# Attention loops of a two-layer transformer: value products in two halves of the queries in three of four steps, side products cut in halves and put in the middle and at the end of steps

## The chip, the cores and the metric

The kernel runs on one core of one Trainium2 chip. The metric is the time of one execution on the device, in microseconds (us). Lower is better.

## The reference, cut to what matters

The input is 16 sequences of 512 tokens with 256 features. Four layers follow each other, each with a normalisation before it and a residual after it: attention, a feed-forward layer, attention with biases, and a layer of decision trees. The change is in the two attentions:

```
q, k, v = h @ w_q, h @ w_k, h @ w_v         # 16 heads of 16 features
s = (q @ k.T) * scale                       # 512 x 512 for each head
e = exp(s - max(s))                         # layer 0: a maximum for each block of 256 keys
out = (e @ v) / sum(e)                      # then out @ w_o, added to x
```

## The kernel before

Two sequences are worked on as a pair, and there are eight pairs. For each pair the program goes through attention of layer 0 on the first sequence (phase 0), on the second (phase 1), both feed-forward layers (phases 2 and 3), attention of layer 1 on both (phases 4 and 5), and the trees (6 and 7). `attention_even` writes phases 0 and 4, `attention_odd` phases 1 and 5, so each runs 16 times. All five engines have their own written order (one function of the same name for each), and semaphores tie them together.

An attention phase has 16 steps s, one for each head. A step has two **pairs of tiles** (`pair_of_tiles`, L1090), one for each half of the keys. A pair is two times: one product of raw scores for a head that lies seven steps ahead (`maxima`, L1033, matmul L1040), whose row maxima VectorE takes out of PSUM (L753 in layer 0, L756 in layer 1), and one product of this head's scores (`scores`, L1049, matmul L1051), which ScalarE turns into exponentials, 1024 columns at a time (`exps`, L518, activation L524). The raw scores have two banks only, so a tile of them can't be written before VectorE has read the tile before the last. The scores of a half wait for the exponentials of the same half one step back. In `attention_even` the tiles ahead belong to the same phase up to step 8 and to the next phase after that. In `attention_odd` there are none from step 9 on.

Between the first and the second pair of a step stand the **value products** of the group of four heads that is done (`weighted`, L1056, matmul L1065): four matmuls, one for each head of the group, each on 32 columns of the array, over 512 queries. In some steps (`split`) they are done over 256 queries between the pairs and over the other 256 after the second pair. bank 6 collects them; after the fourth step of a group ScalarE reads it (`out_read`, L510), in the middle of that step.

After the second pair stand the **side products** of a step, all into bank 7 or banks that are free:

- `attention_even` makes the queries, keys and values of the next phase: `qk_unit` (matmul L1020, six of 512 columns) and `v_unit` (matmul L1001, twelve of 256 columns). ScalarE reads the queries and keys out twice (`qk_read`, L488, activations L494 and L497), GpSimd makes the low part (`qk_low`, L359), and SyncE stacks both parts with DMAs (`stack_up`, L277, issues L284). In phase 4 VectorE reads the values (L743), in phase 0 ScalarE does (L501).
- `attention_odd` finishes the phase before it: `natural` (transposes L1072, four for each of four token tiles), which VectorE divides (L762 and L764), and `attn_T` (transposes L1077), read by `attn_high` and `attn_low`, then the projection.
- Both transpose the split maxima of four heads into rows (`maxima_rows`, L1043, matmul L1046); ScalarE reads them (`row_read`, L508) and SyncE sends them to the score operands (`rows_up`, L287, issues L290). SyncE does this in a written order: the rows for the first group of the odd phase come after `stack_up` of the fourth query or key unit.

TensorE, VectorE and ScalarE each wait in place: what is queued behind a waiting instruction waits too.

Of the kernel before, what the change touches and what calls it, by code (L numbers as in the profile page):

```python
# [13 lines left out]
T = S // P  # L14
# [4 lines left out]
G = 4  # L19
# [36 lines left out]
def build(nc, t, out):  # L56
    ctx = ExitStack()
    with ctx:
# [413 lines left out]
        def _(act):  # L472
# [54 lines left out]
            def attention_even(b, ph):  # L527
                n, nxt = b * NATT + ATT[ph], ph + 1
                for s in range(H):
                    exps(b, ph, s, 0)  # L530
                    if s % G == 3 and s > 3:
                        out_read(n, ph, s // G - 1)
                    exps(b, ph, s, 1)
                    if s % G == 1:
                        row_read(*((n, (s + 3) // G) if s < 13 else (n + 1, 0)))
                    if s == 0 and nxt == 1:
                        hT_high(b, nxt, 0)
                        hT_high(b, nxt, 1)
                    if s in (2, 3) and nxt == 1:
                        qk_read(n + 1, nxt, s - 2)  # L540
                    if s in (1, 2) and nxt == 5:
                        hT_high(b, nxt, s - 1)
                    if s in (3, 4) and nxt == 5:
                        qk_read(n + 1, nxt, s - 3)
                    if s in (7, 8) and nxt < 4:
                        values(n + 1, nxt, s - 7)
                    if s in (11, 12):
                        qk_read(n + 1, nxt, s - 9)

            def attention_odd(b, ph):  # L550
                n, nxt = b * NATT + ATT[ph], ph + 1
                for s in range(H):
# [3 lines left out]
                    if s % G == 3 and s > 3:  # L556
                        out_read(n, ph, s // G - 1)
                    exps(b, ph, s, 1)
                    if s % G == 1 and s < 13:
                        row_read(n, (s + 3) // G)  # L560
                    if s in (8, 9):
                        attn_high(n - 1, ph - 1, s - 8)
                    if s == 14:
# [400 lines left out]
        def _(pe):  # L964
# [104 lines left out]

            def natural(n, ph, tt):  # L1070
                for g in range(NG):
                    i = nc.tensor.transpose(bank[N_BANK[ph][tt]][:, g * P:(g + 1) * P], oT[:, group_at(ph, g), tt * P:(tt + 1) * P], idf[:])  # L1072
                i.then_inc(nat_ps, 1)

            def attn_T(n, ph, k):
                for tt in range(T):
                    i = nc.tensor.transpose(bank[A_BANK[ph][k]][:, tt * P:(tt + 1) * P], nat_h(ph)[:, tt, k * P:(k + 1) * P], idf[:])  # L1077
                i.then_inc(aT_ps, 1)

# [24 lines left out]
            def attention_even(b, ph):  # L1104
                ai, nxt = ATT[ph], ph + 1
                n = b * NATT + ai
                for s in range(H):
# [4 lines left out]
                    pair_of_tiles(b, ph, n, ahead, s, 0)  # L1112
                    split = s in ((4, 5, 9, 13, 14) if nxt == 1 else (5, 9, 13, 14))
                    if s == G and nxt == 1:
                        pe.wait_ge(qk_sb, (n + 1) * 4 + 1)
                    if s >= G:
                        weighted(n, ai, s // G - 1, s % G, (0,) if split else (0, 1))
                    if s == 0 or (s == 1 and nxt == 5):
                        keep_going(4, bank[6])
# [27 lines left out]
                    if s == 4 and nxt == 5:  # L1147
                        pe.wait_ge(qk_sb, (n + 1) * 4 + 1)
                        qk_unit(n + 1, nxt, 1)
                    if s == 5:  # L1150
                        pe.wait_ge(qk_sb, (n + 1) * 4 + 2)
                        maxima_rows(n, 2)
                    if s == 6:
                        pe.wait_ge(mrow_sb, n * NG + 3)
                        v_unit(n + 1, nxt, 0, 0)
                    if s == 7:
                        v_unit(n + 1, nxt, 0, 1)
                    if s == 8:
                        pe.wait_ge(v_sb, (n + 1) * 2 + 1)
                        v_unit(n + 1, nxt, 1)  # L1160
                    if s == 9:
                        pe.wait_ge(v_sb, (n + 1) * 2 + 2)
                        maxima_rows(n, 3)
                    if s == 10:
                        pe.wait_ge(mrow_sb, n * NG + 4)
                        qk_unit(n + 1, nxt, 2, 0)
                    if s == 11:
                        qk_unit(n + 1, nxt, 2, 1)
                    if s == 12:
                        pe.wait_ge(qk_sb, (n + 1) * 4 + 3)  # L1170
                        qk_unit(n + 1, nxt, 3)
                    if s == 13:
# [3 lines left out]
            def attention_odd(b, ph):  # L1176
                ai, nxt = ATT[ph], ph + 1
                n = b * NATT + ai
                for s in range(H):
# [4 lines left out]
                    pair_of_tiles(b, ph, n, ahead, s, 0)  # L1184
                    split = s in (0, 1, 2, 5)
                    values_of = (n - 1, ai - 1, NG - 1, s) if s < G else (n, ai, s // G - 1, s % G)
                    weighted(*values_of, (0,) if split else (0, 1))
                    pair_of_tiles(b, ph, n, ahead, s, 1)
                    if split:
# [3 lines left out]
                    if s == 3:  # L1193
                        pe.wait_ge(mrow_sb, n * NG + 2)
                        pe.wait_ge(oT_sb, n * NG)
                        natural(n - 1, ph - 1, 0)
                    if s == 4:
                        pe.wait_ge(attn_sb, (n - 1) * T + 1)
                        natural(n - 1, ph - 1, 1)
                    if s == 5:  # L1200
                        pe.wait_ge(attn_sb, (n - 1) * T + 2)
                        maxima_rows(n, 2)
                    if s == 6:
                        pe.wait_ge(mrow_sb, n * NG + 3)
                        natural(n - 1, ph - 1, 2)
                    if s == 7:
                        pe.wait_ge(attn_sb, (n - 1) * T + 3)
                        natural(n - 1, ph - 1, 3)
                    if s == 8:
                        pe.wait_ge(attn_sb, (n - 1) * T + T)  # L1210
                        attn_T(n - 1, ph - 1, 0)
                    if s == 9:
# [318 lines left out]
```

## Time and profile before

| | |
|---|---|
| median of 3 runs | 3346.56 us (3345.4 to 3348.39) |
| profiled execution | 3350.38 us, its span 3348.3 us |
| PE busy | 3053.1 us, 91% of the span |
| DVE busy | 2225.5 us, 66% |
| ACT busy | 1915.2 us, 57% |
| POOL busy | 911.7 us, 27% |
| granted TensorE clock, mean | 0.974 of full speed |

PE is TensorE, DVE VectorE, ACT ScalarE, POOL GpSimd, SPq the DMA issues of SyncE. The table gives shares over all stages. How the engines wait for each other within a step has to be read from the timeline.

### The profile page before, as it was taken

Reading aid. Unit: us, or ns where it says so; the run is one execution under the profiler, and the core shown is the slowest. Engines: PE = TensorE matmul, PEld = TensorE weight load, DVE = VectorE, ACT = ScalarE, POOL = GpSimd, SP = SyncE. Lnnn points to the kernel's source line nnn. Section 1 sums busy time; section 2 is a strip of 40 time slices with the busy share of each in tenths; the row PEclk is TensorE's granted clock in tenths of the full one; section 3 lists DMA queues with packets and bytes.
Section 4 is the critical chain, followed back from the end, with each engine's and each line's share of the span. In section 5 each row is a group of like instructions: output and inputs, shape, how many; then the busy total and the mean of one; then the engine's idle time right before and its main releaser. Section 6 shows DMA issues by size and latency. Waiting matters only on the chain.

```text
span 3348.3 us, 51469 instructions
## 1 busy us (share of the span) xinstructions
PE 3053.1 (91%) x20499; PEld 1392.4 (42%) x20499; DVE 2225.5 (66%) x4099; ACT 1915.2 (57%) x2559; POOL 911.7 (27%) x1206
## 2 busy tenths in 40 slices
PE   0489999999999999999999999999999999999999
PEld 0124355242543436333363434524254343633336
DVE  0785866758566675767667586675856667576764
ACT  0265664747557474565746566474754748456574
POOL 0012323141331414214141232314233141421413
PEclk9689999999999999999999999999999999999999
DMA  3000000000010001000010000100001000100000
GB/s 119 21 22 20 22 27 33 22 20 22 31 38 12 23 19 50 28 2 30 24 39 28 18 24 21 39 22 20 22 29 39 12 22 19 47 28 6 30 18 20
DMA packets 92703, 91.08 MB, mean 27 GB/s; under 512 B 15757, under 2 KB 89877, under 8 KB 92453
## 3 DMA queue, kind: packets, MB, share of 16 engines
q1 hardware_dynamic: 92465, 87.79, 7.7%
q8 instruction: 163, 2.67, 0.3%
q14 instruction: 75, 0.61, 0.1%
HBM read 17.48 MB, written 8.39 MB: 8 GB/s over the span
## 4 chain that ended last, share of the span: by engine, by line
PE 63%; DVE 25%; ACT 5%; SPq 3%; issue 2%; POOL 1%; DMA 1%; DVEq 0%
PE ps L995 13%; PE ps L1040 11%; PE ps L1065 11%; PE ps L1271 8%; DVE nmax L756 8%; DVE nmax L753 8%; PE ps L1001 5%; PE ps L1020 4%; PE ps L1242 3%; PE ps L1051 3%; ACT probs L524 3%; SPq L263 2%; DVE h L734 1%; DVE hT L739 1%; PE ps L1008 1%
## 5 line engine op out<-in xcount | busy, mean ns | idle before, releaser
L524 ACT ACTIVATE probs<-ps 128x1024 f32<-128x1024 f32 x1024 | 1042.8, 1025 | 376.1 <-PE ps L1051 371.9
L1040 PE MATMUL ps<-kst,qst 48*128 48x512 f16 x2048 | 719.1, 394 | 114.0 <-DVE nmax L753 50.5
L753 DVE TENSOR_REDUCE nmax<-ps 128x2 f32<-128x512 f32 x1024 | 651.0, 685 | 196.3 <-PE ps L1040 190.8
L756 DVE TENSOR_REDUCE nmax<-ps 128x1 f32<-128x512 f32 x1024 | 651.2, 685 | 175.7 <-PE ps L1040 172.2
L1051 PE MATMUL ps<-qst,kst 54*128 54x512 f16 x2048 | 697.3, 391 | 5.0 <-ACT probs L524 5.0
L1065 PE MATMUL ps<-probs,vn 128*32 128x512 f32 (+1 forms) x5184 | 577.6, 519 | 6.6 <-ACT oT L512 6.6
L1040 PEld LDWEIGHTS ps<-kst,qst 48*128 48x128 f16 x2048 | 164.4, 93 | 734.1 <-DVE nmax L753 308.0
L420 POOL TENSOR_TENSOR probs<-probs 127x512 f16<-127x512 f32 (+1 forms) x256 | 292.4, 1164 | 519.5 <-ACT probs L655 519.5
L655 ACT ACTIVATE probs<-probs 127x512 f16<-127x512 f32 (+1 forms) x256 | 161.7, 632 | 350.2 <-DVE probs L949 346.8
L1271 PE MATMUL ps<-wout,probs 127*128 127x256 f16 (+1 forms) x3072 | 357.2, 273 | 0.0
L995 PE MATMUL ps<-hT,win 128*127 128x512 f16 (+1 forms) x1536 | 354.3, 380 | 2.7 <-ACT probs L631 2.7
L1271 PEld LDWEIGHTS ps<-wout,probs 127*128 127x128 f16 (+1 forms) x3072 | 297.5, 98 | 55.6 <-issue 10.7
L361 POOL TENSOR_TENSOR parts<-qk,parts 128x512 f16<-128x512 f32 x128 | 149.3, 1168 | 409.8 <-ACT qk L497 408.5
L949 DVE SCALAR_TENSOR_TENSOR probs<-ps,thr,probs 127x512 f32<-127x512 f32 (+1 forms) x256 | 179.8, 744 | 121.5 <-PE ps L1262 121.5
L367 POOL TENSOR_TENSOR npart<-nmax,zero 128x32 f16<-128x32 f32 x128 | 30.7, 239 | 796.3 <-DVE nmax L753 456.5
L995 PEld LDWEIGHTS ps<-hT,win 128*127 128x127 f16 (+1 forms) x1536 | 176.4, 117 | 162.8 <-issue 11.5
L631 ACT ACTIVATE probs<-ps,bin_ 128x512 f32<-128x512 f32 (+1 forms) x256 | 162.4, 682 | 94.8 <-PE ps L995 82.6
L1051 PEld LDWEIGHTS ps<-qst,kst 54*128 54x128 f16 x2048 | 157.7, 93 | 121.9 <-issue 79.2
L571 ACT ACTIVATE probs<-ps 128x512 f32<-128x512 f32 x128 | 76.3, 596 | 218.3 <-PE ps L995 218.1
L382 POOL TENSOR_TENSOR probs<-probs 128x512 f32<-128x512 f32 x128 | 132.9, 1041 | 221.1 <-ACT probs L571 221.1
L1065 PEld LDWEIGHTS ps<-probs,vn 128*32 128x32 f32 x5184 | 103.1, 108 | 211.3 <-issue 152.3
L995 PE MATMUL ps<-hT,wfc 128*128 128x512 f16 x768 | 184.7, 380 | 0.0
(117 smaller groups left out, 3282.0 us busy)
## 6 DMA issues: line engine op xcount, KB each, us to landing
qst<-parts SPq DMA_DIRECT2D x384, 64.0 KB, 2.6
kst<-parts SPq DMA_DIRECT2D x384, 64.0 KB, 2.6
x<-in_x SPq DMA_DIRECT2D x16, 512.0 KB, 3.9
probs<-x SPq DMA_DIRECT2D x16, 512.0 KB, 3.0
out<-probs SPq DMA_DIRECT2D x16, 512.0 KB, 3.0
qst<-nrow SPq DMA_DIRECT2D x256, 12.0 KB
qst<-in_winT SPq DMA_DIRECT2D x1, 2040.0 KB
oT<-in_wfcT SPq DMA_DIRECT2D x1, 1024.0 KB
```

The source lines that it names most:

```text
L420: nc.gpsimd.tensor_tensor(mlo[0:rows, a % 2, leaf, :], masked[0:rows, a % 2, leaf, :], mhi[0:rows, a % 2, leaf, :], ALU.subtract).then_inc ...
L524: nc.scalar.activation(probs[:, g % 2, 2 * hf:2 * hf + 2, s % G, :], ps[:, 2 + 2 * hf:4 + 2 * hf, :], ACT.Exp).then_inc(exp_rd, 1)
L631: nc.scalar.activation(actv[0:rows, a % 2, leaf, :], bank[2 + leaf][0:rows], ACT.Silu, scale=1.0 / WS, bias=bin_[0:rows, a % PAR, leaf:lea ...
L753: nc.vector.tensor_reduce(nmax[:, u, 2 * tt + half, :, slot], bank[tt % 2].rearrange("p (a s) -> p a s", s=BLK), AX.X, ALU.max, negate=Tru ...
L756: nc.vector.tensor_reduce(nmax[:, u, 2 * tt + half, 0, slot:slot + 1], bank[tt % 2], AX.X, ALU.max, negate=True).then_inc(max_rd, 1)
L949: nc.vector.scalar_tensor_tensor(masked[0:rows, a % 2, leaf, :], sel_at(a, leaf)[0:rows], thr[0:rows, leaf:leaf + 1], actv[0:rows, a % 2, ...
L995: ins = mm(out_ps, w[:, a, k, col:col + width], src[:, c, k, :], start=k + i == 0, stop=k == KD - 1 and i == 2)
L1001: ins = mm(out_ps, src[:, c, k, tt * P:(tt + 1) * P], w[:, a, k, :], start=k + i == 0, stop=k == KD - 1 and i == 2)
L1040: mm(bank[tt % 2], qst[lo:hi, ai % 2, e // 2, tt * P:(tt + 1) * P], kst[lo:hi, ai % 2, e // 2, :], start=True, stop=True).then_inc(max_ps, 1)
L1051: i = mm(bank[2 + kt], kst[lo:hi, ai % 2, s // 2, kt * P:(kt + 1) * P], qst[lo:hi, ai % 2, s // 2, :], start=True, stop=True)
L1065: i = mm(bank[6][32 * j:32 * j + 32, lo:hi], vn[:, ai % 2, kt, G * g + j, :], probs[:, g % 2, kt, j, lo:hi], start=kt == 0 and 0 in halves ...
L1271: i = mm(bank[4 + tt // 2][:, tt % 2 * D:(tt % 2 + 1) * D], part[0:rows, a % 2, leaf, tt * P:(tt + 1) * P], wout[0:rows, w, c, leaf, :], s ...
```

## The change

In `attention_even` the value products are cut in halves in the first three of every four steps from step 4 on (before: in steps 5, 9, 13, 14, and 4 in phase 0). The fourth step of a group (7, 11, 15) keeps its 512 queries between the pairs. The side products, which stood at the end of their step, whole or in halves, are now all in halves, one at the end of an even step, the other between the pairs of the odd step after it: value units at 6 and 7, 8 and 9, query and key units 2 and 3 at 10 and 11, 12 and 13, and in phase 4 unit 1 at 4 and 5. Step 7 and step 11 so have 512 queries of values and half a unit between their pairs, and nothing after the second. In `attention_odd` the values are cut in steps 0 to 8 except 3 and 7 (before: 0, 1, 2, 5), and each `natural` and the first `attn_T` is cut in two, the first half at the end of a step and the second between the pairs of the next. ScalarE's reads are moved with the products: for a product that is now complete between the pairs of an odd step, the read stands between the two exponentials of step 9, 13 (and 5 in phase 4), and after both at 7 and 11. GpSimd, VectorE and SyncE keep their order.

```diff
@@ ScalarE, attention_even
+                    if s == 5 and nxt == 5:
+                        qk_read(n + 1, nxt, 1)
+                    if s == 9 and nxt == 1:
+                        values(n + 1, nxt, 1)
+                    if s == 13:
+                        qk_read(n + 1, nxt, 3)
                     exps(b, ph, s, 1)
...
-                    if s in (3, 4) and nxt == 5:
-                        qk_read(n + 1, nxt, s - 3)
-                    if s in (7, 8) and nxt < 4:
-                        values(n + 1, nxt, s - 7)
-                    if s in (11, 12):
-                        qk_read(n + 1, nxt, s - 9)
+                    if s == 3 and nxt == 5:
+                        qk_read(n + 1, nxt, 0)
+                    if s == 7 and nxt == 1:
+                        values(n + 1, nxt, 0)
+                    if s == 11:
+                        qk_read(n + 1, nxt, 2)
@@ ScalarE, attention_odd
+                    if s == 9:
+                        attn_high(n - 1, ph - 1, 0)
                     exps(b, ph, s, 1)
...
-                    if s in (8, 9):
-                        attn_high(n - 1, ph - 1, s - 8)
+                    if s == 9:
+                        attn_high(n - 1, ph - 1, 1)
@@ TensorE
-            def natural(n, ph, tt):
-                for g in range(NG):
+            def natural(n, ph, tt, groups=range(NG)):
+                for g in groups:
...
-            def attn_T(n, ph, k):
-                for tt in range(T):
+            def attn_T(n, ph, k, tts=range(T)):
+                for tt in tts:
@@ TensorE, attention_even
-                    split = s in ((4, 5, 9, 13, 14) if nxt == 1 else (5, 9, 13, 14))
+                    split = G <= s and s % G < G - 1
...
+                    if s == 5 and nxt == 5:
+                        qk_unit(n + 1, nxt, 1, 1)
+                    if s == 7:
+                        v_unit(n + 1, nxt, 0, 1)
+                    if s == 9:
+                        v_unit(n + 1, nxt, 1, 1)
+                    if s == 11:
+                        qk_unit(n + 1, nxt, 2, 1)
+                    if s == 13:
+                        qk_unit(n + 1, nxt, 3, 1)
...
-                        qk_unit(n + 1, nxt, 1)
+                        qk_unit(n + 1, nxt, 1, 0)
...
-                    if s == 7:
-                        v_unit(n + 1, nxt, 0, 1)
                     if s == 8:
                         pe.wait_ge(v_sb, (n + 1) * 2 + 1)
-                        v_unit(n + 1, nxt, 1)
+                        v_unit(n + 1, nxt, 1, 0)
...
-                    if s == 11:
-                        qk_unit(n + 1, nxt, 2, 1)
                     if s == 12:
                         pe.wait_ge(qk_sb, (n + 1) * 4 + 3)
-                        qk_unit(n + 1, nxt, 3)
+                        qk_unit(n + 1, nxt, 3, 0)
@@ TensorE, attention_odd
-                    split = s in (0, 1, 2, 5)
+                    split = s < 9 and s % G < G - 1
...
+                    if s in (4, 5, 7, 8):
+                        natural(n - 1, ph - 1, (s - 4) - (s > 6), (2, 3))
+                    if s == 9:
+                        attn_T(n - 1, ph - 1, 0, (2, 3))
                     pair_of_tiles(b, ph, n, ahead, s, 1)
...
-                        natural(n - 1, ph - 1, 0)
+                        natural(n - 1, ph - 1, 0, (0, 1))
...
-                        attn_T(n - 1, ph - 1, 0)
+                        attn_T(n - 1, ph - 1, 0, (0, 1))
```

## Rows read from the trace of the kernel before

**Rows 1.** The page, costliest groups: busy, mean ns, idle before and its releaser
```profile
L524 ACT ACTIVATE probs<-ps 128x1024 f32<-128x1024 f32 x1024 | 1042.8, 1025 | 376.1 <-PE ps L1051 371.9
L1040 PE MATMUL ps<-kst,qst 48*128 48x512 f16 x2048 | 719.1, 394 | 114.0 <-DVE nmax L753 50.5
```

**Rows 2.** Windows of the third pair: length, busy by engine, granted clock, DMA share
```profile
1000.67:1013.19 12.52, 12.17 (x98) 4.19 (x98) 10.21 (x17) 10.10 (x13) 0.99 (x4) 1.00 0.01 2
1013.19:1028.46 15.27, 13.99 (x110) 3.80 (x111) 12.71 (x21) 13.49 (x18) 3.30 (x6) 1.00 0.16 55
1036.65:1057.92 21.27, 20.00 (x153) 6.60 (x149) 18.16 (x34) 16.58 (x19) 1.98 (x8) 1.00 0.01 3
```

**Rows 3.** Timeline, phase 0, step 7 (start, duration, engine, line, idle before in brackets)
```profile
1000.67 0.39 PE L1040 MATMUL ps<-kst,qst 48*128 48x512 f16 x1
1001.12 0.39 PE L1040 MATMUL ps<-kst,qst 48*128 48x512 f16 x1
1001.44 1.06 PE L1065 MATMUL ps<-probs,vn 128*32 128x512 f32 x8
1002.44 0.39 PE L1040 MATMUL ps<-kst,qst 48*128 48x512 f16 x1
1002.66 0.38 PE L1040 MATMUL ps<-kst,qst 48*128 48x512 f16 x1
...
1002.86 2.59 DVE L753 TENSOR_REDUCE nmax<-ps 128x2 f32<-128x512 f32 x4 [0.48 <-PE ps L1040]
1002.97 0.83 PE L1001 MATMUL ps<-wv,hT 128*128 128x256 f16 x6
...
1003.74 0.39 PE L1040 MATMUL ps<-kst,qst 48*128 48x512 f16 x1
```

**Rows 4.** Timeline, phase 0, steps 13 to 15: values over 256 queries, and a row transposition
```profile
1022.08 0.64 PE L1065 MATMUL ps<-probs,vn 128*32 128x256 f32 x8
...
1022.54 0.39 PE L1046 MATMUL ps<-idb,npart 128*24 128x128 f16 x4
...
1022.86 0.39 PE L1040 MATMUL ps<-kst,qst 48*128 48x512 f16 x1
...
1024.94 0.64 PE L1065 MATMUL ps<-probs,vn 128*32 128x256 f32 x8
...
1025.52 0.39 PE L1040 MATMUL ps<-kst,qst 48*128 48x512 f16 x1
```

**Rows 5.** Timeline, phase 0, step 3: a pair of tiles with nothing before it
```profile
989.22 1.89 DVE L753 TENSOR_REDUCE nmax<-ps 128x2 f32<-128x512 f32 x3 [2.33 <-PE ps L1040]
...
989.97 0.39 PE L1040 MATMUL ps<-kst,qst 48*128 48x512 f16 x1 [0.35 <-DVE nmax L753]
...
990.57 0.39 PE L1040 MATMUL ps<-kst,qst 48*128 48x512 f16 x1 [0.21 <-DVE nmax L753]
```

**Rows 6.** Timeline, feed-forward stage: values over 512 queries, then full-array matmuls
```profile
1081.87 1.06 PE L1065 MATMUL ps<-probs,vn 128*32 128x512 f32 x8
...
1082.87 1.05 PE L1242 MATMUL ps<-wpt,probs 128*128 128x256 f16 x8
```

**Rows 7.** Timeline, ScalarE, SyncE and TensorE from the fourth unit to phase 1
```profile
1020.10 0.60 ACT L494 ACTIVATE parts<-ps 128x512 f16<-128x512 f32 x1 [0.35 <-PE ps L1020]
...
1021.74 3.78 SPq L284 DMA_DIRECT2D kst<-parts  x6
1025.57 34.54 SPq L290 DMA_DIRECT2D qst<-nrow  x8
...
1028.46 0.39 PE L1040 MATMUL ps<-kst,qst 48*128 48x512 f16 x1 [0.71 <-DMA qst<-nrow]
```

**Rows 8.** Timeline, phase 1, step 4: VectorE's division and TensorE's transposes; eight transposes
```profile
1041.34 0.25 DVE L762 RECIPROCAL rden<-ps 128x16 f32<-128x16 f32 x1
...
1042.10 0.66 PE L1072 MATMUL ps<-idf,oT 128*128 128x128 f32 x4
...
1042.70 0.39 PE L1040 MATMUL ps<-kst,qst 48*128 48x512 f16 x1
...
1071.11 1.09 PE L1008 MATMUL ps<-idf,h 128*128 128x128 f32 x8
```

More of the change, by code:

```diff
@@ L1068, in weighted @@
                     i.then_inc(pv_step, 1)
-            def natural(n, ph, tt):
-                for g in range(NG):
+            def natural(n, ph, tt, groups=range(NG)):
+                for g in groups:
                     i = nc.tensor.transpose(bank[N_BANK[ph][tt]][:, g * P:(g + 1) * P], oT[:, group_at(ph, g), tt * P:(tt + 1) * P], idf[:])
-                i.then_inc(nat_ps, 1)
-            def attn_T(n, ph, k):
-                for tt in range(T):
+                if g == NG - 1:
+                    i.then_inc(nat_ps, 1)
+            def attn_T(n, ph, k, tts=range(T)):
+                for tt in tts:
                     i = nc.tensor.transpose(bank[A_BANK[ph][k]][:, tt * P:(tt + 1) * P], nat_h(ph)[:, tt, k * P:(k + 1) * P], idf[:])
-                i.then_inc(aT_ps, 1)
+                if tt == T - 1:
+                    i.then_inc(aT_ps, 1)
             def projected(n, ph, half):
@@ L1195, in attention_odd @@
                         pe.wait_ge(oT_sb, n * NG)
-                        natural(n - 1, ph - 1, 0)
+                        natural(n - 1, ph - 1, 0, (0, 1))
                     if s == 4:
                         pe.wait_ge(attn_sb, (n - 1) * T + 1)
-                        natural(n - 1, ph - 1, 1)
+                        natural(n - 1, ph - 1, 1, (0, 1))
                     if s == 5:
@@ L1204, in attention_odd @@
                         pe.wait_ge(mrow_sb, n * NG + 3)
-                        natural(n - 1, ph - 1, 2)
+                        natural(n - 1, ph - 1, 2, (0, 1))
                     if s == 7:
                         pe.wait_ge(attn_sb, (n - 1) * T + 3)
-                        natural(n - 1, ph - 1, 3)
+                        natural(n - 1, ph - 1, 3, (0, 1))
                     if s == 8:
                         pe.wait_ge(attn_sb, (n - 1) * T + T)
-                        attn_T(n - 1, ph - 1, 0)
+                        attn_T(n - 1, ph - 1, 0, (0, 1))
                     if s == 9:
```

## The prediction

> **What bounds the kernel now.** I first read the costliest groups of the page. ScalarE's exponentials idle 376 us, nearly all of it waiting for TensorE's scores; TensorE idles 114 us before the raw score tiles, the largest part released by VectorE's maxima [rows 1]. So TensorE sets the pace of the attention phases, and VectorE can hold it. The windows give the length of the stretches that the change touches, all at the full clock: 12.52 us for steps 7 to 10 of phase 0, 15.27 from step 11 to the start of phase 1, 21.27 for steps 3 to 9 of phase 1 [rows 2]. Last I read single steps in the timeline, for the distances between starts. I count from the first tile of a pair:
>
> - pair: second tile 0.22 later, and the next block 0.32 after the second tile [rows 3].
> - values over 512 queries: 1.00 until the next pair [rows 3]; over 256: 0.58, taken as 0.57 [rows 4].
> - half a side product (six matmuls of 256 columns; three of 512 are the same work): 0.77 until the next pair [rows 3]. Row transposition: 0.32 [rows 4].
> - VectorE starts 0.42 after the pair's first tile when idle [rows 3]. After a read starts, TensorE may write the next tile 0.75 later, and the second tile 1.35 later [rows 5]; I use 0.73 and then steps of 0.62 (2.59 for four tiles, less their tail).
>
> Applied to steps 7 to 10 before, these distances give 3.07 (the start of step 7 to that of step 8 [rows 3]), then a step with a whole unit, a split one with row transposition, and a full one; they sum to the 12.5 of the window [rows 2]. In the old step 7 both halves are full: 0.45 + 0.32 + 1.00 = 1.77 and 0.22 + 0.31 + 0.77 = 1.30. VectorE needs 1.24 for two tiles, is idle 0.48 of each step, and holds TensorE 0.22 once [rows 3].
>
> **The change part by part.** Nothing is taken away: the matmul columns are the same, only four more matmul instructions stand where values are cut, whose cost is in the distances below. What changes is distribution.
>
> (a) Price of a cut. Two halves of values take 2 × 0.57 = 1.14 against 1.00 where each is followed by another kind of matmul. No row shows a half followed by a full-array product. It is followed by a row transposition after 0.46 [rows 4]; 512 queries are followed by a full-array product after 1.00 [rows 6], the same as by a pair [rows 3]. So I take 0.57, and keep 0.46 as the lower bound. The Trainium skill (TensorEngine Tiling (Array Packing), Key Properties) says that changing the tiling mode drains TensorE. By that rule the half pays its drain before a side product too, and the sum would be the higher one below; without it, the lower one.
>
> (b) Steps 6 and 10 of the even phases (cut values, half a unit at the end). Pair at 0, values 0.54; the next pair could come at 1.11, but VectorE began at 0.42 and frees the banks at 1.16 and 1.78. So values at 2.10, side half at 2.67, end at 3.44. Before: 0.54 + 1.00 + 0.55 + 0.77 = 2.86. Costs 0.58 in step 6, where TensorE's waits are back between the pairs and VectorE then idles at the end.
>
> (c) Steps 7 and 11 (512 queries and half a unit in the middle, nothing at the end). Values 0.55, side half 1.55, second pair 2.32, its second tile 2.55. VectorE, idle meanwhile, begins at 2.74, so the next step's pair has its tiles at 3.47 and 4.09, as a pair after a pair in rows 5. Values of step 8 then start at 4.41, where TensorE's work alone would allow 3.4. Step 7 takes 3.47 instead of 3.07.
>
> (d) Steps 8 and 9. From there: second pair 4.98 and 5.33, values 5.65, side half 6.22, step 9 at 6.99; values 7.54, side half 8.11, pair 8.88, values 9.43, rows 9.89, step 10 at 10.20. Here is the gain: the whole unit and the waiting of the old split step 9 are spread. But (c) eats it. Step 10 by (b), with its pair delayed to 10.65: step 11 at 13.63, against 12.52 [rows 2]. +1.1.
>
> (e) Steps 11 to the odd phase. The same up to step 14 (unit 3 ends in the middle of step 13). Its second half starts at 8.11 and ScalarE reads from 8.98, with 0.60 and 0.49 for the two reads; the row transposition behind waits for them until 10.1 and step 14 starts at 10.4. For the DMAs: in the old phase the read of unit 3 starts at 1020.10, the six issues at 1021.74, since SyncE is still busy with unit 2; the rows go out at 1025.57 and TensorE starts phase 1 at 1028.46, released by that DMA [rows 7]. Now: high part ready 9.58, six issues of together 3.8, rows out at 13.4, TensorE 2.9 later at 16.3, against 15.27 [rows 2]. TensorE and VectorE alone would be there at 15.9. +1.0. Queued behind the waiting tile is all of step 0.
>
> Even phase of layer 0: steps 4 and 5 as before, 0.58 + 1.1 + 1.0 = 2.7. Phase 4 has the same and unit 1 in halves at steps 4 and 5: one more cut (0.3), and the row transposition of step 5 now waits for two reads of ScalarE that begin only after the middle product (0.4): 3.4. VectorE's reads of the values there sit in stretches in which it idled; I price them at nothing, 0.2 if that cover fails.
>
> (f) Odd phases, steps 3 to 9. Four transposes take 0.60 until the pair [rows 8]; from eight (1.09) against four (0.66) a half is about 0.45 [rows 8]. Four products are cut in two (+0.3 each, five with attn_T), and values cut in steps 4, 6, 8 (+0.14 each). What VectorE had hidden: in step 4 nothing is lost to the values, but the second pair slips behind the half transposition, VectorE divides (from 1041.34 [rows 8]; about 0.62 until its next tile) and the tiles behind it come later. Worked through from step 3: steps 4 to 10 start at 2.95, 6.30, 9.39, 12.59, 15.90, 19.43 and, since the row transposition of step 9 now waits for ScalarE's and VectorE's reads of the first attn_T (made in the middle of the step), 23.1, against 21.27 [rows 2]. +1.8; with 0.46 and a half transposition at 0.33, +0.8. From step 10 on the work is the same and TensorE-bound; nothing is given back.
>
> **Sum.** 2.7 + 3.4 + 2 × 1.8 = 9.7 us for a pair of sequences, × 8 = 78 us. On the profiled execution's 3350.4: 3428. The median of the runs lies 3.8 below it, so 3424. Bounds: with the low prices 1.9 + 2.3 + 2 × 0.8 = 5.8, × 8 = 46, 3393; with a SyncE chain of 4.5 instead of 3.8 and 2.2 in an odd phase 3.4 + 3.7 + 4.4 = 11.5, × 8 = 92, 3439.
>
> **Rivals.**
>
> (A) Faster. The single waits of TensorE for a bank, 0.2 to 0.4 us in steps 7, 8, 9, 11, 12 and 13 of an even phase (1.6 together; the 0.22 of step 7 is in rows 3), vanish because cut values keep VectorE supplied earlier, while the six cuts cost 0.14 each: -0.8 for a phase, × 32 phases = -26 us, 3321. It decides for this if a bank is free when TensorE comes back, thus if VectorE lags less than 1.1 behind a pair. For: VectorE idles 0.48 in a step [rows 3], scores come sooner, and ScalarE waits for them [rows 1]. Against: rows 5 show 1.35 until the second tile.
>
> (B) No change. What TensorE loses in (b) and (c) it regains in (d), since VectorE's and TensorE's totals are the same and the cuts hide in waits: 3346. For: steps 8 and 9, taken alone, are as long as before. Against: (c) leaves a pair against a pair, a wait that no other work covers, and the odd phases have no such pair to regain from.
>
> (C) Slower through the clock. TensorE is now about 85% busy in steps where it was 93%. If the granted clock falls to 1.2 GHz in steps 7 and 11, the matmuls after it double for a while: a lost 1.1 us for each six matmuls, twice in each of 32 phases, +70 on top: 3490. Against: the clock is 1.00 in all three windows, split steps with waits among them [rows 2].
>
> **How the numbers follow.** Forecast 0.80 (slower by 46 to 92), C 0.06, A 0.08, B 0.06. Slower by over 0.2% (6.7 us, about what a measurement of this kernel can tell from no change): 0.86; within 0.2%: 0.06; faster: 0.08. The range runs from 3375, below the low prices, since one of the waits may be covered, to 3450.
>
> **What would show it.** In the changed profile, step 7 of phase 0: after the second pair VectorE starts 0.42 later, and the next pair's tiles follow 1.15 and 1.77 after the pair, released by VectorE; steps 7 to 10 last 13.6. TensorE's idle before L1040 grows from 114 us to some 170. Phase 1 starts 16.3 after step 11, released by the DMA of the rows. Half values to half a unit: 0.57 (right) or 0.46. Steps 3 to 9 of the odd phase: 23 instead of 21.3. I am wrong if step 7 is 3.1 or less, or if the banks are free when TensorE comes back from half the values.

## The result, and the profile after

The changed kernel takes 3427.8 us (median of 4, 3424.0 to 3434.6) against 3347.5 us: slower by a factor of 1.0231 (95% interval 1.0214 to 1.0247), 80 us. The forecast was 3424, of a range of 3375 to 3450. The profiled execution of the changed kernel took 3431.0 us, its span is 3428.9 us.

The page of the changed kernel, busiest engines and the groups that answer to those of [rows 1] (busy, mean ns, idle before and its releaser):

```profile
PE 3098.3 (90%) x21459; PEld 1403.2 (41%) x21459; DVE 2231.0 (65%) x4099; ACT 1923.1 (56%) x2559; POOL 911.8 (27%) x1206
...
L524 ACT ACTIVATE probs<-ps 128x1024 f32<-128x1024 f32 x1024 | 1042.3, 1026 | 436.2 <-PE ps L1059 432.8
L1048 PE MATMUL ps<-kst,qst 48*128 48x512 f16 x2048 | 718.7, 397 | 137.3 <-DVE nmax L761 55.3
```

TensorE has 960 matmul records more (the cut values: 480 matmuls of the program, of which the profile shows two records each) and is busy 45 us longer, 3098.3 against 3053.1. The span grew by 80.6, so the other 35 are idle time. Busy time isn't all work, as shown below: short waits hide in it. ScalarE idles 60 us longer before its exponentials, waiting for scores.

The windows of the third pair, those of [rows 2] and in the same order: length, then busy by engine (PE, PEld, DVE, ACT, POOL), granted clock, DMA share:

```profile
1024.86:1038.41 13.55, 12.68 (x114) 4.37 (x113) 10.27 (x16) 10.29 (x12) 0.98 (x4) 1.00 0.01 2
1038.41:1054.62 16.21, 14.22 (x118) 3.75 (x119) 12.59 (x20) 13.24 (x17) 3.31 (x6) 1.00 0.15 51
1062.80:1085.74 22.94, 21.11 (x177) 6.93 (x173) 18.50 (x34) 17.03 (x19) 1.98 (x8) 1.00 0.01 3
```

Steps 7 to 10 of phase 0 last 13.55 us instead of 12.52, step 11 to the start of phase 1 16.21 instead of 15.27, steps 3 to 9 of phase 1 22.94 instead of 21.27. The clock is full in all six. In the first and the last, TensorE's busy time grew by 0.51 and 1.11 and its idle time by 0.52 and 0.56.

That can't be read as work and waiting. The record of a score tile lasts 0.39 us, while the next one may start 0.22 us after it, so the profile shows a wait only from the end of the record on. The two tiles of the second pair of step 6 in the changed kernel:

```profile
1022.61 0.39 PE L1048 MATMUL ps<-kst,qst 48*128 48x512 f16 x1
...
1023.20 0.39 PE L1048 MATMUL ps<-kst,qst 48*128 48x512 f16 x1 [0.21 <-DVE nmax L761]
```

The second comes 0.59 after the first, 0.37 later than it could, and 0.21 of that is shown as idle. What is work and what is waiting is taken from distances between starts at the end of the experiments.

Step 7 of phase 0 in the changed kernel, to the values of step 8 (start, duration, engine, line; idle before in brackets), to be laid beside [rows 3]:

```profile
1023.52 0.64 PE L1073 MATMUL ps<-probs,vn 128*32 128x256 f32 x8
1024.09 0.83 PE L1009 MATMUL ps<-wv,hT 128*128 128x256 f16 x6
...
1024.86 0.39 PE L1048 MATMUL ps<-kst,qst 48*128 48x512 f16 x1
...
1025.39 1.07 PE L1073 MATMUL ps<-probs,vn 128*32 128x512 f32 x8
...
1026.39 0.83 PE L1009 MATMUL ps<-wv,hT 128*128 128x256 f16 x6
...
1027.15 0.39 PE L1048 MATMUL ps<-kst,qst 48*128 48x512 f16 x1
...
1027.57 3.95 DVE L761 TENSOR_REDUCE nmax<-ps 128x2 f32<-128x512 f32 x6 [1.01 <-PE ps L1048]
...
1028.41 0.37 PE L1048 MATMUL ps<-kst,qst 48*128 48x512 f16 x1 [0.66 <-DVE nmax L761]
...
1028.92 0.39 PE L1048 MATMUL ps<-kst,qst 48*128 48x512 f16 x1
```

VectorE had nothing to do for 1.01 us while TensorE did values and half a unit. Then the second pair comes at 1027.15, and the pair of step 8, with nothing between, can't start before VectorE has read: at 1028.41, 1.26 after it, and its second tile 1.77 after it. Step 7 lasts 3.55.

### The profile page after: what moved, and what is told of

The parts are those of the page before. It is cut to its first block, busy times and chain, and to the rows that moved or that the text cites. A ratio compares the mean times of both kernels' runs of the same rounds, so it can differ in the third digit from the quotient of the medians.

```text
span 3428.9 us, 53389 instructions
## 1 busy us (share of the span) xinstructions
PE 3098.3 (90%) x21459; PEld 1403.2 (41%) x21459; DVE 2231.0 (65%) x4099; ACT 1923.1 (56%) x2559; POOL 911.8 (27%) x1206
## 4 chain that ended last, share of the span: by engine, by line
PE 65%; DVE 21%; ACT 5%; SPq 4%; issue 2%; DMA 1%; POOL 1%; DVEq 0%
PE ps L1003 13%; PE ps L1073 12%; PE ps L1048 11%; PE ps L1293 8%; DVE nmax L761 6%; DVE nmax L764 6%; PE ps L1028 5%; PE ps L1009 5%; PE ps L1264 3%; PE ps L1059 2%; SPq L263 2%; ACT probs L524 2%; SPq L284 2%; PE ps L1080 1%; DVE h L742 1%
## 5 line engine op out<-in xcount | busy, mean ns | idle before, releaser
L1073 PE MATMUL ps<-probs,vn 128*32 128x256 f32 (+1 forms) x6144 | 602.1, 465 | 6.6 <-ACT oT L512 6.6
L1073 PEld LDWEIGHTS ps<-probs,vn 128*32 128x32 f32 x6144 | 122.0, 108 | 263.8 <-issue 205.1
```

The lines of the kernel that those rows point to most:

```text
L1073: i = mm(bank[6][32 * j:32 * j + 32, lo:hi], vn[:, ai % 2, kt, G * g + j, :], probs[:, g % 2, kt, j, lo:hi], start=kt == 0 and 0 in halves ...
```

## The experiments

All times are medians. Each kernel ran on one chip together with the kernel before, whose median there is given too, since it differs by some 6 us from chip to chip. Most of the differences between steps are in this table, the distances between the first score tiles of steps 6 to 14 of phase 0 and steps 3 to 9 of phase 1 (medians of eight pairs, us):

```
phase 0, step     6     7     8     9    10    11    12    13    14
before         2.85  3.07  3.74  2.86  2.85  3.07  3.74  2.86  2.66
cuts_only      3.42  2.85  4.08  2.86  3.41  2.85  4.06  2.86  2.66
sides_only     2.85  3.79  3.12  3.43  3.07  3.82  3.12  3.69  2.66
whole change   3.42  3.56  3.41  3.18  3.41  3.55  3.40  3.43  2.66
step7_end      3.42  2.85  3.42  3.18  3.41  2.85  3.42  3.43  2.66
nine_mid       2.85  3.07  3.09  3.43  3.07  3.09  3.09  3.69  2.66

phase 1, step     3     4     5     6     7     8     9
before         3.07  2.99  3.01  3.09  3.18  2.96  2.98
cuts_only      3.07  3.25  2.99  3.27  3.08  3.23  2.97
sides_only     2.89  3.67  3.33  3.09  3.85  3.44  3.71
whole change   2.89  3.24  3.33  3.05  3.47  3.24  3.70
attnT_back     2.89  3.24  3.33  3.05  3.47  3.46  2.98
```

**Which loop.** `even_only` and `odd_only` take the change in one attention function (ScalarE's and TensorE's) and leave the other as before.

> The change in attention_even alone, attention_odd as before. Theory (waits at the raw-score banks, priced by place): the 16 even phases carry 2.7 and 3.4 us each, 49 us together, so about 3347 + 49 = 3396. Rival (the clock: 115 us of the changed kernel's profile are at the lower clock after the start against 75 before, in steps 1 to 3 of the even phases, which the change does not touch): the loss follows the clock; with 40 us more at half speed, some 20 us of it would come or go whichever loop is changed, and the even phases at full clock would carry only about 35.

> The change in attention_odd alone. Theory: 16 odd phases at 1.7 us (the profile of the changed kernel shows 46.9 against 45.2 where the clock stays up), 27 us, about 3375; steps 3 to 9 last 22.9 us against 21.3. Rival (the losses of the two loops are not separate, an odd phase is late because the even phase before hands its rows over late): nearly nothing here, below 8 us, 3350 to 3355.

Measured: 3394.3 us for the even loop and 3376.2 for the odd one, before 3353.6: +41 and +23 (1.0124, interval 1.0109 to 1.0140, and 1.0077, 1.0059 to 1.0094). Both carry a loss of their own; the shapes of their steps are those of the whole change to 0.02 us, the rival that an odd phase only inherits its lateness is out. The sum, 64, lies below 80. In the profiled executions the part of the even loop is 43 us and that of the odd loop 25 by the starts of the phases. The whole change has some 10 us more in the first steps of the phases, which it doesn't touch and where the clock was lower (below).

**Cuts or places.** `cuts_only` has the new `split` conditions and nothing else; `sides_only` the moved and halved side products with the old ones:

```diff
# cuts_only, against the kernel before
-                    split = s in ((4, 5, 9, 13, 14) if nxt == 1 else (5, 9, 13, 14))
+                    split = G <= s and s % G < G - 1
...
-                    split = s in (0, 1, 2, 5)
+                    split = s < 9 and s % G < G - 1
# sides_only, against the changed kernel: the same four lines the other way round
```

> Only the value products are cut in more steps, in both loops; all side products and reads stay where they were. Theory: a cut step with a side product at its end costs 0.57 us (steps 6 and 10), 0.3 where the product is whole (8 and 12), 1.7 for an even phase, and about 1.2 for an odd one: 28 + 19 = 47 us, about 3394. Rival (the cost of a cut is its switch alone, 0.14 us each, waits do not come with it): 4 cuts in an even phase and 3 in an odd one, 112 in all, 16 us: 3363.

> The side products and their reads are moved and cut as in the change, but the values are cut only in the steps in which they were before. Theory: steps 7 and 11 of an even phase last 3.5 instead of 3.07 (a pair after a pair), steps 8 and 9 win a little, the end of the phase is later by unit 3's later reads: 1.0 to 1.3 us for an even phase; 0.8 to 1.2 for an odd one: 29 to 40 us in all, 3377 to 3387. Together with the cuts alone about the 80 us of the whole. Rival (cuts cost all, places nothing): within 7 us of before, 3340 to 3354.

Measured: cuts alone 3380.8 against 3353.6, +27 (1.0084, 1.0069 to 1.0099). Side products alone 3432.2 against 3351.9, +80 (1.0243, 1.0225 to 1.0261): as much as the whole change. Both expectations missed, in opposite directions. The table shows why. A cut at step 6 costs 0.57, as expected, but step 7 gets back 0.22 of it: its second tile no longer waits. And the moved side products alone are worse at steps 7, 9, 11 and 13 than with the cuts, for the same reason. Step 7 of `sides_only`:

```profile
1014.50 0.39 PE L1048 MATMUL ps<-kst,qst 48*128 48x512 f16 x1
...
1014.95 0.39 PE L1048 MATMUL ps<-kst,qst 48*128 48x512 f16 x1
...
1017.03 0.39 PE L1048 MATMUL ps<-kst,qst 48*128 48x512 f16 x1
...
1018.29 0.37 PE L1048 MATMUL ps<-kst,qst 48*128 48x512 f16 x1 [0.66 <-DVE nmax L761]
```

Here the second tile comes 0.45 after the first; in the whole change it follows at 0.22. The distance rule behind both: the second tile of a pair can't come before 1.77 after the first tile of the pair before (0.42 until VectorE starts, 1.35 until its second bank is free). A half step shorter than 1.55 waits for the difference, and a longer one gives nothing back. The kernel before has halves of 1.30 and 1.77, and waits 0.22 a step. With cuts and a half unit at the end (step 6 of the whole change) the lengths are 1.18 and 2.24, with everything in the middle (step 7) 2.29 and then 1.26. With the side products moved, the cuts of the values so cost nothing on top. Taken the other way round the cuts cost 27 and the places 53 more: the two don't add up, and the share of each depends on the order in which they are counted. The loops differ too: by the table, steps 6 to 14 of phase 0 are 0.5 us longer in the whole change than in `sides_only`, steps 3 to 9 of phase 1 are 1.05 us shorter.

**Is it the pair after a pair?** `step7_end` is the whole change, with the second halves of the units at steps 7 and 11 back at the end of those steps.

```diff
-                    if s == 7:
-                        v_unit(n + 1, nxt, 0, 1)
...
-                    if s == 11:
-                        qk_unit(n + 1, nxt, 2, 1)
...
+                    if s == 7:
+                        v_unit(n + 1, nxt, 0, 1)
...
+                    if s == 11:
+                        qk_unit(n + 1, nxt, 2, 1)
```

> The whole change, but the half units of steps 7 and 11 go back to the end of their step, so that no pair of tiles directly follows a pair. Theory: step 7 is 2.9 instead of 3.56 us and step 8 about the same, 0.6 to 0.7 us won at two places of 16 phases, 19 to 22 us: about 3407; TensorE's wait of 0.66 us for VectorE at the start of step 8 is gone. Rival (what costs is the number of cuts, the place of the side product does not matter): within 5 us of the changed kernel, 3423 to 3433.

Measured: 3402.0 against 3353.6 (1.0147, 1.0132 to 1.0163). The excess over the kernel before is 48 us instead of 80, somewhat more than the 22 expected to go. Step 7 is 2.85 instead of 3.56 and step 11 the same, 1.4 us for a phase or 22 in all; the two excesses come from two chips. The two profiled executions differ by 29 us: 19 in the steps that the change touches, 9 in steps 0 to 3 of phase 0 and 0 to 2 of phase 1, which neither touches and where the changed kernel had the lower clock. The window of step 7 (second line: that of steps 7 to 10) shows TensorE busy to the end:

```profile
1013.22:1016.07 2.85, 2.85 (x23) 0.96 (x23) 2.18 (x4) 2.18 (x3) 0.00 (x0) 1.00 0.00 0
1013.22:1026.09 12.87, 12.67 (x115) 4.42 (x115) 10.31 (x16) 10.24 (x12) 0.98 (x4) 1.00 0.01 2
```

12.67 busy, as in the whole change, in 12.87 instead of 13.55 us. The idle time is 0.20 us, less than the 0.35 of the kernel before [rows 2]: the waiting that the change adds here is gone, what the pieces cost remains.

**Is VectorE the cause of the waits?** In `before_halfmax` and `after_halfmax` the maxima are taken over half of the columns only; the other half of the scores is left out of the maxima.

```diff
-  nc.vector.tensor_reduce(nmax[...], bank[tt % 2].rearrange("p (a s) -> p a s", s=BLK),
+  nc.vector.tensor_reduce(nmax[...], bank[tt % 2].rearrange("p (a s) -> p a s", s=BLK)[:, :, 0:BLK // 2],
...
-  nc.vector.tensor_reduce(nmax[...], bank[tt % 2],
+  nc.vector.tensor_reduce(nmax[...], bank[tt % 2][:, 0:BLK],
```

> The kernel before with VectorE's maxima taken over half of the columns of each tile (the other half is left out of the computation), so that one read takes about 0.42 instead of 0.685 us and frees its bank earlier. Theory: the small waits of TensorE for a bank (0.2 us in full steps, 0.4 in split ones) and the VectorE-bound steps at the start of each phase go: 40 to 90 us faster, about 3280. Rival (VectorE is not what holds TensorE): 3347.

> The changed kernel with the same halved maxima. It is to be compared with the kernel before with halved maxima. Theory: the waits for banks go, what stays of the change is the switch of each cut, 0.14 us for 7 more cuts of values in an even and an odd phase together plus cut side products, about 0.3 to 0.4 us for each, and the later reads: 1.2 to 2 us for two phases, 16 of them: the difference to the kernel before with halved maxima falls from 80 to 20 to 35 us. Rival (cuts and switches cost it, or the DMA and ScalarE reads): the difference stays at 60 us or more.

Measured: 3188.1 and 3250.8, against 3351.9 for the kernel before (0.9513 and 0.9701). VectorE does hold TensorE, and by 164 us, more than I thought. But the difference between the two is 63 us, where my theory said 20 to 35: here it fell. The windows of steps 7 to 10 of phase 0 and 3 to 9 of phase 1, first of `before_halfmax`, then of `after_halfmax`:

```profile
954.23:965.79 11.56, 11.56 (x99) 3.87 (x99) 6.05 (x16) 9.99 (x13) 0.98 (x4) 1.00 0.01 2
987.52:1006.51 18.99, 18.72 (x152) 6.34 (x148) 12.10 (x34) 16.45 (x19) 1.96 (x8) 1.00 0.02 4
```
```profile
967.41:979.85 12.44, 12.05 (x115) 4.30 (x115) 6.05 (x16) 9.95 (x12) 0.98 (x4) 1.00 0.01 2
1002.23:1023.20 20.97, 20.14 (x176) 6.65 (x172) 12.20 (x34) 16.88 (x19) 1.96 (x8) 1.00 0.01 4
```

The first stretch is without any idle time in the kernel before, and has 0.39 us in the changed one; it is 0.88 longer there, and 1.03 with full maxima. The pair after the pair of step 7 is still 1.00 apart (1.26 with full maxima), since the 0.42 until VectorE starts doesn't shrink with the read. In the odd phase the loss isn't smaller but larger, 1.98 against 1.67. So halving the reads does not take the changed kernel's waits for the banks away, and the 63 us can't be called the part without VectorE.

The runs show another thing. The kernel before and `before_halfmax` issue the same matmuls, and in steps 7 to 10, at the full clock in both, TensorE is busy 12.17 us in one [rows 2] and 11.56 in the other; on the page it is 3053.1 against 2947.3. So busy time holds waits for VectorE.

**The read in step 9 of the odd phases.** `attnT_back` is the whole change with the first `attn_T` whole at the end of step 8 and read there:

```diff
-                    if s == 9:
-                        attn_T(n - 1, ph - 1, 0, (2, 3))
...
-                        attn_T(n - 1, ph - 1, 0, (0, 1))
+                        attn_T(n - 1, ph - 1, 0)
# ScalarE: attn_high in steps 8 and 9, after the second exponentials, as before
```

> The whole change, but the first attn_T of the odd phases stands whole at the end of step 8 again and ScalarE reads it there. Theory: of the 1.65 us that steps 3 to 9 of an odd phase are longer in the changed kernel, 0.7 are step 9 (3.70 against 2.98), where the row transposition waits for ScalarE's and VectorE's reads of a product made only in the middle of the step; they go, 0.2 come back at the end of step 8 for the longer block there: 16 phases at 0.5 to 0.7 us, 8 to 11 us faster than the changed kernel, 3417 to 3420. Rival (the odd phases' loss is the raw-score banks and cut values, the reads are hidden): within 4 us of the changed kernel.

Measured: 3420.0 against 3350.7 (1.0207, 1.0192 to 1.0222), 8 us below the changed kernel's time, on another chip; the intervals of the two ratios still overlap. The steps show where: step 9 falls from 3.70 to 2.98 and step 8 rises from 3.24 to 3.46, 0.50 us for each of 16 phases. In the changed kernel VectorE's low part ends that chain:

```profile
1083.56 0.44 PE L1086 MATMUL ps<-idf,h 128*128 128x128 f32 x2
1083.93 0.60 PE L1059 MATMUL ps<-qst,kst 54*128 54x512 f16 x2
1084.04 0.60 ACT L516 ACTIVATE hT<-ps 128x512 f16<-128x512 f32 x1 [0.34 <-PE ps L1086]
1084.46 0.66 PE L1086 MATMUL ps<-idf,h 128*128 128x128 f32 x4
...
1084.67 0.69 DVE L778 TENSOR_TENSOR hT<-ps,hT 128x512 f16<-128x512 f32 x1 [2.09 <-ACT hT L516]
1085.41 0.39 PE L1054 MATMUL ps<-idb,npart 128*24 128x128 f16 x4 [0.29 <-DVE hT L778]
```

**Is one idea of the change good by itself?** `nine_mid` is the kernel before, with the whole units of steps 8 and 12 cut, the second half between the pairs of steps 9 and 13, and their reads moved as in the change. Nothing else is cut.

```diff
-                        v_unit(n + 1, nxt, 1)
+                        v_unit(n + 1, nxt, 1, 0)
...
-                        qk_unit(n + 1, nxt, 3)
+                        qk_unit(n + 1, nxt, 3, 0)
...
+                    if s == 9:
+                        v_unit(n + 1, nxt, 1, 1)
+                    if s == 13:
+                        qk_unit(n + 1, nxt, 3, 1)
```

> The kernel before with one idea of the change alone: the whole unit at the end of steps 8 and 12 is cut, and its second half goes between the pairs of steps 9 and 13, which have cut values already. Nothing else is cut and no pair follows a pair. Theory, by the distances: steps 8 to 10 last 3.07 + 3.20 + 3.07 = 9.34 instead of 9.45 us, twice in 16 phases, less what unit 3's later reads cost at the end of the phase (0 to 0.5): between 4 us faster and 4 us slower, 3343 to 3351. Rival (moving the read of unit 3 to the middle of step 13 makes SyncE and the rows late): 1 us for each even phase, 3363.

Measured: 3364.5 against 3351.9 (1.0040, 1.0027 to 1.0052), 13 us slower, and a miss. The rival's number came out (3363), its reason in part. Steps 8 and 10 are at the 3.07 to 3.09 that I expected, step 9 is 3.43 where I had 3.20: I had forgotten that its pair's second tile waits to 1.77 after the pair before (0.46 instead of 0.22). Step 13 is 3.69, since its second tile waits likewise and the row transposition behind it waits for ScalarE's reads of unit 3 (0.25 of it). Together 0.3 us by steps 8 to 14 and 0.3 more until phase 1, which is the rival's late hand-over of the rows: 10 us of the 13.

**The clock.** In steps 1 to 3 of the even phases, in which the change moves nothing (the units of these steps stay whole), the granted clock falls in both kernels. Phase 0 of the third pair, steps 1 to 3, in the kernel before and in the changed one:

```profile
980.39:992.29 11.90, 8.92 (x41) 2.54 (x41) 8.71 (x15) 8.62 (x12) 2.14 (x5) 0.86 0.06 19
```
```profile
1001.92:1015.69 13.77, 11.20 (x41) 2.80 (x41) 8.89 (x15) 8.62 (x12) 2.14 (x5) 0.66 0.08 27
```

The same 41 matmuls last 1.9 us longer at a mean clock of 0.66. That is in the 80 us and in no step of the change. To take out as much of it as possible, `before_warm` and `after_warm` issue the score products of these steps twice; TensorE waits for VectorE there and has room.

```diff
             def scores(n, ai, s, kt):
                 lo, hi = s % 2 * HALF, s % 2 * HALF + KROWS
+                for _ in range(1 if ai % 2 == 0 and s in (1, 2, 3) else 0):
+                    mm(bank[2 + kt], kst[lo:hi, ...], qst[lo:hi, ...], start=True, stop=True)
```

> The kernel before, with the score products of steps 1 to 3 of the even phases issued twice (the second writes the same values), so that TensorE idles less in the stretch in which the clock was seen to fall. Theory: the extra work is 0.85 us in each of three steps, partly inside waits for VectorE; if the clock stays up, steps 3 and 4 are as short as their shortest (3.5 and 3.5 instead of 5.2 and 4.5 in phase 4): between 10 us faster and 15 us slower. Rival: the clock falls as often, and the doubled products cost 20 us or more.

> The changed kernel with the same doubled score products, to be compared with the kernel before with them. Theory (places and waits): 70 us or more slower than that one, as the clock is no part of it. Rival (the clock): the difference falls to 60 us, since the 40 us more at the lower clock are gone from the changed kernel.

Measured: 3329.8 and 3410.7, against 3349.3 on the same chip. The kernel before gets 19.5 us faster (0.9944, 0.9927 to 0.9961), more than expected, and so does the changed one, by some 17. The difference of the two is 81 us, as without the doubled products, so the rival's 60 us is out. The clock isn't the same in the two, though: its mean is 0.985 in `before_warm` and 0.981 in `after_warm`, whose steps 0 to 3 of phase 0 and 0 to 2 of phase 1 are together 10 us longer over the eight pairs. In the steps from there on, which the change touches, the loss is 73 us, against 69 without the doubled products. So the change costs some 70 us with the clock up, and some 10 more came in both pairs of kernels with a lower clock ahead of these steps. Why the changed kernel gets the lower clock there stays open. Steps 2 to 5 of phase 4 of the second pair, in the kernel before and in `before_warm`:

```profile
760.80:776.41 15.61, 14.13 (x77) 3.80 (x77) 11.60 (x19) 11.25 (x15) 3.31 (x6) 0.78 0.10 35
```
```profile
753.98:767.15 13.17, 12.81 (x85) 3.71 (x85) 11.49 (x19) 11.17 (x15) 3.29 (x6) 1.00 0.11 38
```

Eight matmuls more take 2.4 us less, at 1.00 instead of 0.78. `before_warm2` issues the products three times in steps 1 and 2 of phase 0:

> The kernel before with the score products doubled in steps 1 to 3 of phase 4 as in the earlier run (20 us faster than before), and issued three times in steps 1 and 2 of phase 0, once in step 3. Theory: in phase 4 the clock no longer falls and steps 3 and 4 gain 2.4 us (437.6 to 421.5 us over the eight phases); in phase 0 the doubled products left one fall of 3.4 us in half of the phases, so a fuller TensorE before the first query unit (5.3 us in the kernel before, 4.9 where the clock stays up) may gain up to 0.5 us for each: 20 to 24 us faster than before. Rival (phase 0 is bound by VectorE there, filler only lengthens it): 10 to 16 us faster.

Measured: 3331.3 against 3350.7 (0.9941, 0.9927 to 0.9954). In its profiled execution the clock is full in all attention phases but the first, and phase 0 is 0.8 us shorter than in `before_warm` (410.9 for 417.0 over eight); the medians of the two can't be told apart. The gain, 19.4 us, is just below the 20 to 24 that I expected, and not the rival's 10 to 16; more filler than in `before_warm` shows no gain beyond it.

**Work and waiting, by the distances.** For every block of matmuls and the kind of block behind it, I take the shortest distance between their starts at the full clock in these traces (2% may lie below) as work, and what a distance has above it as waiting. This is an estimate, worked out from all starts in the steps that the change touches (even phases from step 4 on, odd phases steps 3 to 9). In us for all 32 phases, above the kernel before (last line: `after_halfmax` above `before_halfmax`); raw tiles includes the wait for the rows at the start of an odd phase:

```
                 longer   work   waits: raw tiles   row transposition   other
cuts_only          29      17         10                   0               2
sides_only         79      12         40                  15              12
whole change       69      29         25                  15               1
step7_end          50      32          1                  15               2
halved maxima      68      29         18                  15               6
```

Of the 25 us before the raw tiles, 6 are the late rows in front of an odd phase and 19 are VectorE's banks; `step7_end`, without a pair directly behind a pair, has none of the 19. The 15 are row transpositions that wait in steps 13, 5 (phase 4) and 9 (odd phases) for ScalarE's and VectorE's reads of a product made in the middle of the step. The 29 are the pieces: 0.14 for each cut of values, about 0.10 for each cut unit, 0.18 for each `natural` cut in two. The cuts add 17 of work to the moved side products and save 27 of waiting, which is why they seem free there.

## Why the prediction came out

The forecast was 78 us more, measured are 80. By its own steps:

- **(a) The cut.** Half values to half a unit: 0.57 (1023.52 to 1024.09 above), as taken, not 0.46. A cut so costs 2 × 0.57 − 1.00 = 0.14. The Trainium skill (TensorEngine Tiling (Array Packing), Key Properties) says that a change of the tiling mode drains TensorE. The trace agrees in that a half pays 0.57 before a full-array product too; no run shows whether a drain is what the 0.14 consists of.
- **(b) to (d)** Step 6: 3.42 (I had 3.44). Step 7: 3.55 (3.47). The next pair's tiles 1.26 and 1.77 after the pair (1.15 and 1.77). Steps 7 to 10: 13.55 (13.63). The first of the two release distances was 0.1 too short.
- **(e)** Step 11 to phase 1: 16.21 (16.3). The chain is the predicted one, read late, six issues, rows out, TensorE:

```profile
1047.33 0.60 ACT L494 ACTIVATE parts<-ps 128x512 f16<-128x512 f32 x1 [0.27 <-PE ps L1028]
...
1047.95 3.73 SPq L284 DMA_DIRECT2D kst<-parts  x6
...
1051.73 1.57 SPq L290 DMA_DIRECT2D qst<-nrow  x2
...
1054.62 0.39 PE L1048 MATMUL ps<-kst,qst 48*128 48x512 f16 x1 [0.94 <-DMA qst<-nrow]
```

- **(f)** Steps 3 to 9 of the odd phase: +1.67 (I had 1.8), 0.72 of it in step 9. Half a transposition takes 0.37 until the next tiles (1083.56 to 1083.93 above) and not 0.45.
- **Phase 4** was put at 3.4; where the clock stays up in both (`before_warm` and `after_warm`) it is 55.5 against 52.5 us, 3.0. Steps 7 to 11 lost less there, since the kernel before waits more around VectorE's reads of the values.

At the full clock these make 2.6 + 3.0 + 2 × 1.67 = 8.9 for a pair of sequences, 72 us. The other 9 are the clock's lower stretches in the first steps of phases, which came longer in the changed kernel's profile than in that of before, and which I had put at nothing in the forecast (rival C placed a fall in steps 7 and 11; there is none). So two misses of some 6 and 9 us hide each other, and the hit to 4 us is partly luck.

What was wrong in the reasons: I said that TensorE's idle time in front of the raw tiles would grow from 114 to 170 us; it is 137. The page counts idle time only behind the end of a record, so part of each wait is hidden. And I headed the account with waiting for VectorE. By the distances the pieces are the largest part, 29 us; VectorE's banks take 19, row transpositions behind late reads 15, the late rows 6, and the clock ahead of these steps some 10. All but the clock stand in the steps of my sum, at about their size, so the mechanism was right in its parts and not in which of them is the largest. It differs by phase: in steps 7 to 10 of phase 0 waiting is 0.7 of the 1.03 us, in steps 3 to 9 of phase 1 the pieces are 1.1 of the 1.67. Rival A was right in one point: cut values do save a wait, 0.22 in the step after, which is part of why the whole change is no slower than its side products alone.

## What to carry to other kernels

Where a producer and its reader share two banks, take the distance from one block of two tiles to the next: here the second tile comes no earlier than 1.77 us after the first tile of the block before. Spread other work so that each gap is just filled, since a gap that is too long pays nothing back for one that is too short; of the splits tried in a step with whole values, half a side product in the middle and nothing at the end was the worst. And price a cut by what it adds to the distance between starts on the engine that sets the pace (here 0.14 us for each cut of values), before counting what it may hide. Busy time on the page is no measure of it, since short waits count as busy there.

## What the runs showed of the hardware

- Work added in a stretch in which TensorE waited for VectorE made the kernel 19.5 us faster, since the granted clock stayed at 1.00 instead of 0.78 over steps 2 to 5 of phase 4: 13.17 instead of 15.61 us with eight matmuls more.
- Where the clock falls isn't fixed by the code nearby: steps 1 to 3 of phase 0 have the same instructions in both kernels, and for the third pair ran at 0.86 in one and 0.66 in the other.
- VectorE starts 0.42 us after the first tile of a pair whether it reads 512 or 256 columns of each, so that a pair directly behind a pair comes 1.00 us after it with half the columns and 1.26 with all.
- TensorE's busy time in the profile holds waits: with the same matmuls and the full clock it is 11.56 us instead of 12.17 over steps 7 to 10 of phase 0 when VectorE's reads are halved, since a record of a score tile lasts 0.39 us and the next may start after 0.22.
